# Row maxima of causal attention from 64-row matmuls, two heads at a time, with two score banks and four maximum banks

## The reference

```python
scores = jnp.einsum('bqhd,bkhd->bhqk', q, k)                                  # 16 heads, 32 channels each
scores = scores + jnp.einsum('bqr,bkr->bqk', q_rope, k_rope)[:, None]         # 32 rotary channels shared by the heads
scores = scores / scale
scores = jnp.where(causal[None, None], -jnp.inf, scores)
w = jax.nn.softmax(scores, axis=-1)
attn = jnp.einsum('bhqk,bkhd->bqhd', w, v).reshape(Bb, Tt, D_MODEL)
```

## Time and profile before

| | |
|---|---|
| median of 3 runs | 4271.21 us (4269.56 to 4274.83) |
| profiled execution: its own time | 4269.43 us |
| profiled execution: span | 4267.3 us |
| mean granted clock of TensorE | 0.941 of full speed |
| busy in the span: PE / DVE / POOL / ACT | 3893.6 / 2801.9 / 2434.3 / 1775.5 us |
| attention loop, 560 to 3392 us: PE / DVE / POOL / ACT busy | 2632.7 / 1832.0 / 1817.0 / 1324.5 us of 2832 |
| one unit, 736.9 to 914.2 us: PE / DVE / POOL / ACT busy | 164.2 / 116.6 / 113.6 / 83.0 us of 177.3 |
| last unit, 3226 to 3392 us: PE busy | 147.9 us of 166 |

### The profile page before, as it was taken

The page is one execution under the profiler, slowest core; times in us unless marked ns, Lnnn a source line. Parts: engine busy times, 40 slices in busy tenths (PEclk is TensorE's granted clock), DMA queues, the critical chain, the costliest instruction groups (busy, mean ns, idle before and its releaser), DMA issues. The chain is left out here.

```text
span 4267.3 us, 71588 instructions
## 1 busy us (share of the span) xinstructions
PE 3893.6 (91%) x20832; PEld 2495.9 (58%) x20832; DVE 2801.9 (66%) x4366; ACT 1775.5 (42%) x3401; POOL 2434.3 (57%) x1149
## 2 busy tenths in 40 slices
PE   7999689989889999999988999999999789999998
PEld 4777455555555555555555555555555367777777
DVE  5667465767657676576765767657676267777776
ACT  2333134545445454444544545444454423333333
POOL 2333146657566675666756657566576645555555
PEclk9999789999999999899999999999999889999999
DMA  5888845253452534525345253452532211111110
GB/s 185 287 286 285 244 94 114 51 118 75 92 115 50 121 75 90 114 51 117 73 95 115 51 118 71 96 114 51 117 70 58 84 60 59 59 61 60 66 59 30
DMA packets 239115, 440.97 MB, mean 103 GB/s; under 512 B 25396, under 2 KB 26932, under 8 KB 238648
## 3 DMA queue, kind: packets, MB, share of 16 engines
q1 hardware_dynamic: 238776, 436.74, 39.5%
HBM read 301.90 MB, written 134.23 MB: 102 GB/s over the span
## 5 line engine op out<-in xcount | busy, mean ns | idle before, releaser
L823 DVE TENSOR_REDUCE att_piece_max<-att_ps_m 128x1 f32<-128x512 f32 (+3 forms) x2560 | 1485.1, 606 | 901.0 <-PE att_ps_m L933 458.9
L787 ACT ACTIVATE att_probs<-att_ps_s 128x512 f32<-128x512 f32 (+3 forms) x2560 | 1287.0, 533 | 1498.9 <-PE att_ps_s L950 1450.0
L895 POOL TENSOR_TENSOR att_sum_g<-att_sum_g,att_probs 128x2048 f32<-128x2048 f32 (+3 forms) x384 | 1441.4, 3754 | 198.2 <-ACT att_probs L787 158.9
L949 PE MATMUL att_ps_s<-att_q_a,att_k_a 128*128 128x512 f32 (+3 forms) x2560 | 1028.2, 406 | 106.3 <-issue 87.9
L950 PE MATMUL att_ps_s<-att_q_b,att_k_b 65*128 65x512 f32 (+3 forms) x2560 | 956.2, 378 | 0.0
L931 PE MATMUL att_ps_m<-att_k_a,att_q_a 128*128 128x512 f32 (+3 forms) x1792 | 681.0, 399 | 19.0 <-DVE att_piece_max L823 19.0
L956 PE MATMUL att_ps_o<-att_probs,att_v 128*32 128x512 f32 (+3 forms) x5120 | 607.3, 547 | 57.0 <-POOL att_probs L873 57.0
L949 PEld LDWEIGHTS att_ps_s<-att_q_a,att_k_a 128*128 128x128 f32 x2560 | 510.9, 200 | 246.7 <-issue 156.1
L931 PEld LDWEIGHTS att_ps_m<-att_k_a,att_q_a 128*128 128x128 f32 x1792 | 341.5, 195 | 348.4 <-DVE att_piece_max L823 202.8
L950 PEld LDWEIGHTS att_ps_s<-att_q_b,att_k_b 65*128 65x128 f32 x2560 | 504.4, 197 | 65.6
L873 POOL TENSOR_SCALAR_AFFINE_SELECT att_probs<-att_probs 128x512 f32<-128x512 f32 x256 | 162.2, 634 | 555.2 <-ACT att_probs L787 555.2
(11 more groups left out here) (176 smaller groups left out, 5169.9 us busy)
## 6 DMA issues: line engine op xcount, KB each, us to landing
att_q_a<-s_q_hi SPq DMA_DIRECT2D x128, 256.0 KB, 4.8
att_q_a<-s_qr_hi SPq DMA_DIRECT2D x128, 256.0 KB, 5.5
prj_x_sb<-in_x_dram SPq DMA_DIRECT2D x16, 1024.0 KB, 5.3
s_q_hi<-prj_q_hi SPq DMA_DIRECT2D x16, 1024.0 KB, 4.4
s_q_lo<-prj_q_lo SPq DMA_DIRECT2D x16, 1024.0 KB, 6.4
s_k_hi<-prj_k_hi SPq DMA_DIRECT2D x16, 1024.0 KB, 6.7
s_k_lo<-prj_k_lo SPq DMA_DIRECT2D x16, 1024.0 KB, 7.6
s_v<-prj_v_sb SPq DMA_DIRECT2D x16, 1024.0 KB, 8.7
```

Source lines behind the costliest of these rows:

```text
L787: act.activation(probs[s % RING][:, hh, c0:CH], ps_s[(GH * s + hh) % SBANKS][:, c0:CH], ACT.Exp, scale=SCALE).then_inc(probs_ready, 1)
L823: dve.tensor_reduce(piece_max[:, j, hh * TB + r, kc:kc + 1], ps_m[:, bank, 0:width], AX_X, ALU.max).then_inc(piece_taken, 1)
L895: pool.tensor_tensor(sum_g[:, :, c0:CH], sum_g[:, :, c0:CH], new, ALU.add).then_inc(sum_added, 1)
L949: mm(out[:, c0:CH], k_a[:, hh, i * P:(i + 1) * P], q_a[j][:, hh, c0:CH], start=True, stop=False)
```

## The change

A piece of the row maxima becomes a pair: the same query tile and key chunk for two heads at once. Each head's matmul has 64 rows (k high against q high alone) and so a tile of half the array: even heads on rows 0 to 63, odd heads on rows 64 to 127, each into a bank of its own. For that, keys of odd heads are stored with high and low halves exchanged, in `k_a` and `k_next`, which makes 10 DMAs of a key load where there were 6, and 8 where there were 4. The row maximum is thereby one of the products of the high halves. The scores themselves stay as they were; a softmax doesn't depend on what exactly is subtracted from its exponents.

There are 80 pairs in a unit instead of 160 pieces, 32 of them diagonal. The mask matmul L933 is gone. DVE takes an off-diagonal pair in one reduction of 128 x 2 x 512; in a diagonal pair it makes one `tensor_tensor_reduce` for each head, which adds a mask of [128, 512] (fp32, from SBUF) to the columns in PSUM, writes the sum back to PSUM and gives the row's maximum (`keep["mask_qk"]` grows to that size). `att_ps_m` has 2 slots of 2 banks, `att_ps_s` 2 banks. PV stands between the second and the third score tile of the next step. The last pass visits its key chunks in the order 1, 0, 2, 3 (`key_tile`), and the pairs of (2, kc = 1) join those made ahead: 40 pairs ahead, 40 in the unit itself. `max_schedule` deals by an estimated time of DVE for each pair (`cost`) against a new `room`.

```diff
-SBANKS = 3
-MBANKS = 3
+SBANKS = 2
+MSLOTS = 2
+KR = HD + DR
@@
+def key_tile(j, i):
+
+    return i ^ TB if j == TCH - 1 and i < 2 * TB else i
+
 def max_pieces(j):
 
-    return [(j, hh, r, kc) for kc in range(j + 1) for hh in range(GH) for r in range(TB)]
+    return [(j, hp, r, kc) for kc in range(j + 1) for hp in range(GH // 2) for r in range(TB)]
 
 def for_next(item):
 
-    return item[0] < 2 or (item[0] == 2 and item[-1] == 0)
+    return item[0] < 2 or (item[0] == 2 and item[-1] in (0, 1))
+
+def cost(item):
+
+    return 5 if item[-1] < item[0] else 3 + item[2]
@@ load_k and load_k_next of SP
+            def load_keys(dst, i, done):
+
+                for odd in range(2):
+                    hi_at, lo_at = (KR, 0) if odd else (0, KR)
+                    for row, src in ((hi_at, heads["k_hi"][i]), (hi_at + HD, rotary("kr_hi", i)),
+                                     (lo_at, heads["k_lo"][i]), (lo_at + HD, rotary("kr_lo", i))):
+                        sp.dma_start(as_f32(dst[row:row + HD, odd::2, :]), src[:, odd::2, :]).then_inc(done, 16)
@@ maxima of DVE
-                    _, hh, r, kc = item
-                    width = CH if kc < j else (r + 1) * P
-                    dve.tensor_reduce(piece_max[:, j, hh * TB + r, kc:kc + 1], ps_m[:, bank, 0:width], AX_X,
-                                      ALU.max).then_inc(piece_taken, 1)
+                    _, hp, r, kc = item
+                    if kc < j:
+                        first = 2 * hp * TB + r
+                        dve.tensor_reduce(piece_max[:, j, first:first + TB + 1:TB, kc], ps_m[:, slot, :, :], AX_X,
+                                          ALU.max).then_inc(piece_taken, 1)
+                    else:
+                        width = (r + 1) * P
+                        for odd in range(2):
+                            at = (2 * hp + odd) * TB + r
+                            last = dve.tensor_tensor_reduce(ps_m[:, slot, odd, 0:width], ps_m[:, slot, odd, 0:width],
+                                                            keep["mask_qk"][:, CH - width:CH], 1.0, MASKED, ALU.add, ALU.max,
+                                                            piece_max[:, j, at, kc:kc + 1])
+                        last.then_inc(piece_taken, 1)
@@ maximum of PE
                 width = CH if kc < j else (r + 1) * P
-                keys = k_next[:, hh, 0:width] if for_next(item) and kc == 0 else k_a[:, hh, kc * CH:kc * CH + width]
-                last = mm(ps_m[:, bank, 0:width], q_a[j][:, hh, r * P:(r + 1) * P], keys, start=True, stop=(kc < j))
-                if kc == j:
-                    last = mm(ps_m[:, bank, width - P:width], keep["ident_b"][:], keep["mask_qk"][:], start=False, stop=True)
+                for odd in range(2):
+                    hh, rows = 2 * hp + odd, slice(KR * odd, KR * odd + KR)
+                    keys = k_next[rows, hh, 0:width] if for_next(item) and kc == 0 else k_a[rows, hh, kc * CH:kc * CH + width]
+                    last = mm(ps_m[:, slot, odd, 0:width], q_a[j][rows, hh, r * P:(r + 1) * P], keys, start=True, stop=True)
                 last.then_inc(piece_ready, 1)
@@ body of PE
-                    parts = [lambda hh=hh: scores(u, j, i, hh) for hh in range(GH) if s < NSTEP]
+                    parts = [lambda: scores(u, j, i, 0), lambda: scores(u, j, i, 1), lambda: scores(u, j, i, 2),
+                             lambda: scores(u, j, i, 3)] if s < NSTEP else [lambda: None]
                     if before:
-                        parts.append(lambda: weighted_values(u, *before))
+                        parts.insert(2, lambda: weighted_values(u, *before))
                     items = kept_items(s, nxt)
-                    if s == NSTEP:
-                        parts = [lambda: None] * (len(items) - 1) + parts
+                    cut = [0, 1, 1, 2, 2] if s < NSTEP else [0, 0]
                     for n, part in enumerate(parts):
                         part()
-                        for it in items[len(items) * n // len(parts):len(items) * (n + 1) // len(parts)]:
+                        for it in items[cut[n]:cut[n + 1] if n + 1 < len(parts) else None]:
```

More of the change, by code:

```diff
@@ L587, in max_schedule @@
     own = [it for it in pieces[2] if not for_next(it)] + pieces[3]
-    ahead = pieces[0] + [it for it in pieces[2] if for_next(it)] + pieces[1]
-    for items, steps in ((own, range(1, 22)), (ahead, range(23, NSTEP + 1))):
-        seen, done = 0, 0
+    ahead = pieces[0] + [it for it in pieces[2] if for_next(it) and it[-1] == 0] + pieces[1] \
+        + [it for it in pieces[2] if for_next(it) and it[-1] == 1]
+    for items, steps in ((own, range(0, 22)), (ahead, range(23, NSTEP + 1))):
+        seen, done, spent = 0, 0, 0
         for s in steps:
             seen += room(s)
-            upto = len(items) * seen // sum(map(room, steps))
-            plan[s] += items[done:upto]
-            done = upto
+            share = sum(map(cost, items)) * seen / sum(map(room, steps))
+            while done < len(items) and spent + cost(items[done]) / 2 <= share:
+                spent += cost(items[done])
+                plan[s].append(items[done])
+                done += 1
+        assert done == len(items)
     for j in range(TCH):
         last = max(s for s in plan if pieces[j][-1] in plan[s])
-        plan[min(last + 1, NSTEP)].append((j, "turn"))
+        if j == TCH - 1:
+            plan[last + 2].insert(0, (j, "turn"))
+        else:
+            plan[last + 1].append((j, "turn"))
     return plan
@@ L717, in load_k_next @@
             def load_k_next(u):
-                i = TCH * u
-                for row, src in ((0, heads["k_hi"][i]), (HD, rotary("kr_hi", i)),
-                                 (2 * HD, heads["k_lo"][i]), (3 * HD, rotary("kr_lo", i))):
-                    sp.dma_start(as_f32(k_next[row:row + HD, :, :]), src).then_inc(kn_in, 16)
+                load_keys(k_next[:], TCH * u, kn_in)
             def load_v(u, j):
@@ L906, in loads, with key_loads @@
                 return 6 * 16 * (u + 1)
+            def key_loads(u):
+                return 10 * 16 * (u + 1)
             def maximum(unit, item, place, u):
-                j, bank = item[0], place % MBANKS
-                if place >= MBANKS:
-                    used = place - MBANKS
-                    if NAHEAD <= place < NAHEAD + MBANKS:
-                        used = max(used, max(p for p in range(NAHEAD, NAHEAD + NPIECE) if p % MBANKS == bank) - NPIECE)
+                j, slot = item[0], place % MSLOTS
+                if place >= MSLOTS:
+                    used = place - MSLOTS
+                    if NAHEAD <= place < NAHEAD + MSLOTS:
+                        used = max(used, max(p for p in range(NAHEAD, NAHEAD + NPIECE) if p % MSLOTS == slot) - NPIECE)
                     pe.wait_ge(piece_taken, NPIECE * unit + used + 1)
@@ L918, in maximum @@
                     pe.wait_ge(max_ready, TCH * u + j + 1)
-                    pe.transpose(ps_m[0:GH * TB, bank, 0:P], row_max[:, j, :], keep["ident_f"][:]).then_inc(piece_ready, 1)
+                    pe.transpose(ps_m[0:GH * TB, slot, 0, 0:P], row_max[:, j, :], keep["ident_f"][:]).then_inc(piece_ready, 1)
                     return
-                _, hh, r, kc = item
-                if hh == 0 and r == 0:
+                _, hp, r, kc = item
+                if hp == 0 and r == 0:
                     if kc == 0:
@@ L945, in scores @@
                 if i == TB * j and hh == 0:
-                    need.append((k_in[j], loads(u)))
+                    need.append((k_in[j], key_loads(u)))
                 waits(pe, *need)
                 out = ps_s[bank]
-                mm(out[:, c0:CH], k_a[:, hh, i * P:(i + 1) * P], q_a[j][:, hh, c0:CH], start=True, stop=False)
-                last = mm(out[:, c0:CH], k_b[:, hh, i * P:(i + 1) * P], q_b[j][:, hh, c0:CH], start=False, stop=True)
+                keys = slice(key_tile(j, i) * P, (key_tile(j, i) + 1) * P)
+                mm(out[:, c0:CH], k_a[:, hh, keys], q_a[j][:, hh, c0:CH], start=True, stop=False)
+                last = mm(out[:, c0:CH], k_b[:, hh, keys], q_b[j][:, hh, c0:CH], start=False, stop=True)
                 last.then_inc(scores_ready, 1)
@@ L973, in weighted_values @@
                     pe.wait_ge(v_in[j], 16 * u + 16)
-                last = over_keys(ps_o, lambda hh: v[:, i // TB, i % TB, hh * HD:(hh + 1) * HD], probs[s % RING],
+                kc, kt = divmod(key_tile(j, i), TB)
+                last = over_keys(ps_o, lambda hh: v[:, kc, kt, hh * HD:(hh + 1) * HD], probs[s % RING],
                                  start=(i == 0), stop=(i == STEPS[j] - 1), c0=c0)
```

48 lines of the change are left out of this document (27 added, 21 removed).

## The result

| | before | after |
|---|---|---|
| median | 4272.12 us (4269.56 to 4274.83) | 4735.61 us (4717.28 to 4742.15) |
| profiled execution: time / span | 4269.43 / 4267.3 us | 4717.28 / 4715.5 us |
| mean granted clock | 0.941 | 0.872 |
| period of a unit (median in the trace) | 177.3 us | 205.7 us |

The ratio is 1.1078, 95% interval 1.1044 to 1.1112: 11% slower. 16 units by 28.4 us are 454 of the 463 us, so nearly the whole loss lies in the attention loop. The forecast was 4268, its range ended at 4560.

A forecast was written before the change was run, and what follows sets the result against it. PE was taken to set the pace. Terms -23.4 + 12.8 + 9 + 1 gave -0.6 us a unit, -10 over 16 units; with +6 outside, -4 against 4269.4, so 4268 us, range 4150 to 4560.

The forecast's parts named there:

- Term 1: PE's own work: pair halves run side by side without drains, mask matmuls go; -23.4 us a unit.
- Term 2: Two score banks: PE's score tiles wait for the exponential some 40 times a unit; +12.8 us a unit.
- Term 3: Masked steps: with less PE work ahead of the last PV, PE waits for POOL's chain; +9 us a unit.
- Term 4: DVE's reductions and masked maxima: DVE stays at 115 to 125 us of 177, doesn't bind; +1 us a unit.
- Term 5: Outside the loop's steady state: prelude +10 us once for its maxima, last unit -4 once.
- Rival A: PE: each change of the row tile drains, 0.39 us per lone pair; +17 us a unit, 4540; chance 0.27.

The follow-up runs named there:

- short sums: POOL's additions in the masked steps cut to 16 columns a head, part of the sums left out: changed kernel 4462 us, kernel before 4205 us.
- e6: Changed kernel with pairs over all 128 rows and PV behind the fourth score tile: 4273 us, ratio 1.0009 to the kernel before.

## Why the prediction was wrong

- *What bounds the kernel* was right: PE does, before and after.
- *Term 1, -23.4*: this is the step that failed. "I take the projection's row, since it is single-pass against single-pass as the pairs are." What changes there is the size in columns, and that is free; the change between 128 and 64 rows costs 0.39 for a lone pair, at prices that stood around PV, though PV changes columns and passes and not rows. That the halves run side by side was right. At 0.39 for 54 lone pairs and 0.2 for the rest it comes to about +3 instead of -23, by estimate. The runs that isolate the row tile say that 64-row pairs are 8.2 to 8.4 us a unit dearer than pairs over all rows, where term 1 had them 16 cheaper (11.1 and 4.9, the streaming saved). Also in term 1, the 7.7 us for the mask matmuls didn't come in the kernel before: taking them out alone changed nothing (0.9991), and with an even deal it gave 1.3 us a unit (173.2 and 171.9).
- *Term 2, +12.8*: the waits are there (42 a unit); two banks cost 8.1 in the kernel before, with PV last. Within the change they weren't measured apart.
- *Term 3, +9*: the place was right, the path incomplete. The waits come to 2.6 us more at PE in the changed kernel and 7 with PV in the middle alone, but the clock falls with them. POOL's chain and what hangs on it are 13.7 in the kernel before with PV in the middle and 12.4 of the changed kernel's loss. Term 3 had the clock at nothing, and no rival had it, although show a whole unit at 0.95 and a stretch at 0.50, and the trace before has the fall at 726 behind a wait of 1.11 us for POOL. This is the second step that failed.
- *Term 4*: DVE busy 116.2 us a unit, as forecast (115 to 125). The reduction of 1,024 columns takes 1.221 us (forecast 1.22), the masked one of 512 columns 0.715, its read 0.141.

```profile
L852 DVE TENSOR_REDUCE att_piece_max<-att_ps_m 128x2 f32<-128x1024 f32 x744 | 900.6, 1221 | 706.8 <-PE att_ps_m L973 706.6
L858 DVE CUSTOM_DVE_ANT_0 att_ps_m<-att_ps_m,mask_qk 128x512 f32<-128x512 f32 x248 | 166.9, 715 | 122.2 <-PE att_ps_m L973 122.2
L858 DVE DVE_READ_ACCUMULATOR2_ANT att_piece_max<- 128x1 f32 x992 | 140.2, 141 | 0.0
```

- *Term 5*: the loop's first score tile starts at 560.75 us, 0.9 us later than before (559.86); +10 was wrong, and why stays open.
- *Rival A* had the right price of a drain and gave 4540. What it lacks to 4736 is about 12 us a unit. The clock, which A doesn't have, is the likeliest source: it falls further when drains and waits come together (61 us a unit at 1.2 GHz against 26 and 30, and 9.4 us of time more than the two give singly). It wasn't isolated.
- *Open*: of the 16.0 us between the changed kernel and the one before, both with short sums (190.0 and 174.0), 8.2 to 8.4 are the row tile. The other 7.6 aren't assigned. They are near the two banks' 8.1, but with PV last two banks and all the rest sum to nothing (e6); so it would have to be two banks together with PV in the middle, the case of term 2. That PV's place costs 0.1 with short sums was measured with three banks only. Three score banks beside the four of the maxima and the two of the outputs would be nine, where both kernels use eight; neither this nor all rows with PV in the middle and short sums was tried.

## What to carry to other kernels

Half-height matmuls for two heads at once don't pay when they stand singly between full-height ones: count each change of the row tile, both sides of it, against the streaming saved (here 0.39 against 0.23 for a pair of 512 columns). Two such pairs in a row would save 0.46 for the same 0.39, an estimate from these rows; grouping wasn't tried. Before moving work that waits for another engine forward, look what stands ahead of it, and look at the clock row as well as at the waits: here the sum of the waits said neither what the move cost (7 us of 13.7) nor what waits alone cost (5.3 us a unit for 0.1). Work that can be dealt freely is worth dealing evenly, so that no engine gets much of it at once; here that alone was worth 1.5%, and with the masks on DVE 2.1%, but with 64-row pairs and PV in the middle nothing.

## What the runs showed of the hardware

- A change of rows (128 to 64 and back) between single-pass matmuls costs 0.09 us going in and 0.20 coming out, and 0.11 for the next load, at full clock. From 128 rows to 65 nothing is paid (0.23, L990 to L991), and a change of columns doesn't cost either: 0.23 in the projection. After the turn (L959, 128 rows, 16 columns) the score matmul starts 0.03 later, while the turn itself comes 0.43 after a pair:

```profile
1154.65 0.50 PE L973 MATMUL att_ps_m<-att_k_a,att_q_a 64*128 64x512 f32 x2
1155.08 0.28 PE L959 MATMUL att_ps_m<-ident_f,att_row_max 128*16 128x128 f32 x1
1155.11 0.43 PE L990 MATMUL att_ps_s<-att_q_a,att_k_a 128*128 128x384 f32 x1
```

- TensorE's granted clock fell from 1.00 to 0.50 in masked steps around waits of 1.1 to 1.9 us, and in the changed kernel mostly stayed there for 17 to 24 us. It didn't take the idle end of a unit. Work that was of no use made the kernel with PV in the middle 0.9% faster by the medians (4456 from 4497 us), at 11% of the time at 1.2 GHz instead of 23%.
- Waits in sum aren't time lost: 85.7 us of PE's waits for POOL in place of 0.6 left the period at 174.1 in place of 174.0 us.
